# A four-attention chain on one core: the fourth attention's residual and norm moved to token-major rows, epsilon moved into the sum of squares, the last tail in halves, a new order

## What is computed

```python
# block 0: self-attention (sa), strided cross-attention (ca), feed-forward (f), each followed by a LayerNorm
# block 1 (l1): cross-attention, update, LayerNorm:
x4 = (x - mu) * rsqrt(var + 1e-05) * ln_gamma + ln_beta
# block 2 (l2, g): causal cross-attention, residual with its input, LayerNorm, feed-forward
sim = softmax(where(causal, Q @ K^T / sqrt(8), -1e9))
att_h = (sim @ V) + x4                    # V = ctx @ Wv.T + bv
mu, var = mean(att_h), mean((att_h - mu) ** 2)
x5 = (att_h - mu) * rsqrt(var + 1e-05) * ln_g + ln_b
x6 = gelu(x5 @ W1.T + b1) @ W2.T + b2 + x5
# block 3 (l3): attention with squared relu scores in a band, no softmax, then the output
out = x6 + (w / max(sum(w), 1e-06)) @ V @ Wo.T
```

## Time and profile before

| | before |
|---|---|
| median of 3 runs | 197.07 us (196.1 to 197.6) |
| the profiled execution's own time | 196.68 us |
| span of its profile, first to last instruction | 194.7 us |
| granted TensorE clock | 1.000 of full speed |
| busy: PE, PEld | 177.8 us (91%), 134.4 us (69%) |
| busy: DVE, ACT, POOL | 129.3 (66%), 118.1 (61%), 37.5 (19%) us |
| matmul records | 4559 |

### The profile page before, as it was taken

How to read it: one execution, slowest core, us unless ns; L and a number is a source line. 1 busy time by engine, 2 the same in 40 slices (tenths; PEclk the granted TensorE clock), 3 DMA queues, 4 the chain that set the end, 5 groups by cost and what they waited for, 6 DMA issues and landing times.

```text
span 194.7 us, 10288 instructions
## 1 busy us (share of the span) xinstructions
PE 177.8 (91%) x4559; PEld 134.4 (69%) x4559; DVE 129.3 (66%) x251; ACT 118.1 (61%) x307; POOL 37.5 (19%) x65
## 2 busy tenths in 40 slices
PE   7688899988999999999999997979899999999954
PEld 3466577867778699688777574656667677787743
DVE  4899869745865774693679372867855425778850
ACT  3466535774768866567844754365688575757442
POOL 8800007163303024201111100230100101100000
PEclk9999999999999999999999999999999999999999
DMA  5994000000000000000000000000000000000102
GB/s 134 323 389 160 5 3 8 3 3 3 3 3 3 3 3 2 2 3 3 3 3 7 3 5 3 3 3 3 3 5 3 3 3 3 3 0 7 32 3 81
DMA packets 4187, 6.05 MB, mean 31 GB/s; under 512 B 560, under 2 KB 3504, under 8 KB 3888
## 3 DMA queue, kind: packets, MB, share of 16 engines
q1 hardware_dynamic: 3712, 5.23, 8.1%
q10 hardware_dynamic: 432, 0.17, 0.3%
HBM read 4.88 MB, written 0.52 MB: 28 GB/s over the span
## 4 chain that ended last, share of the span: by engine, by line
PE 78%; DVE 7%; issue 6%; ACT 4%; DMA 2%; POOL 0%; ACTq 0%; POOLq 0%
PE bank L334 36%; PE score L337 22%; PE bank L337 12%; PE bank L557 5%; DVE m_col_sb L911 4%; DMA small_sb<-in_small 2%; ACT probs_sb L699 2%; ACT v_ext_sb L683 1%; DVE probs_sb L898 1%; PE bank L467 1%; DVE k_heads_sb L830 1%; DVE q_heads_sb L852 1%; PE bank L415 1%; ACT probs_sb L749 1%; PE bank L620 0%
## 5 line engine op out<-in xcount | busy, mean ns | idle before, releaser
L911 DVE TENSOR_REDUCE m_col_sb<-score 128x32 f32<-128x2048 f32 (+1 forms) x16 | 30.2, 1890 | 11.8 <-PE score L337 11.7
L699 ACT ACTIVATE probs_sb<-score 128x1024 f32<-128x1024 f32 (+1 forms) x28 | 26.2, 963 | 13.1 <-PE score L337 13.0
L334 PEld LDWEIGHTS bank<-v_ext_sb,probs_sb 128*32 128x32 f32 x2176 | 23.1, 110 | 11.4 <-issue 8.5
L334 PE MATMUL bank<-v_ext_sb,probs_sb 128*32 128x18 f32 (+1 forms) x2176 | 27.2, 189 | 2.6 <-issue 1.4
L1042 POOL TENSOR_SCALAR vare_sb<-var_sb 128x2 f32<-128x2 f32 x20 | 7.0, 352 | 106.7 <-ACT att_sb L756 106.7
L337 PE MATMUL score<-q_heads_sb,k_kept_sb 32*64 32x256 f32 x512 | 19.4, 386 | 1.5 <-issue 1.1
L334 PE MATMUL bank<-xa_sb,W_sb 128*128 128x256 f32 x62 | 18.0, 399 | 1.7 <-issue 1.0
L756 ACT ACTIVATE att_sb<-bank 128x128 f32<-128x128 f32 x40 | 10.7, 275 | 10.9 <-PE bank L337 10.8
L557 PE MATMUL bank<-W_sb,att_sb 128*128 128x128 f32 x80 | 16.0, 287 | 0.7 <-DVE att_sb L939 0.4
L1044 POOL TENSOR_TENSOR rstd_sb<-vare_sb,half_sb 128x2 f32<-128x2 f32 x20 | 15.6, 778 | 1.7
L337 PE MATMUL score<-k_heads_sb,q_kept_sb 32*64 32x256 f32 x384 | 13.8, 383 | 2.1 <-issue 1.3
(11 more groups left out here) (143 smaller groups left out, 341.7 us busy)
## 6 DMA issues: line engine op xcount, KB each, us to landing
W_sb<-in_mats SPq DMA_DIRECT2D x1, 1088.0 KB, 8.3
W_sb<-in_mats SPq DMA_DIRECT2D x1, 1024.0 KB, 10.4
ctxT_sb<-in_ctxT SPq DMA_DIRECT2D x1, 512.0 KB, 6.1
cn_sb<-in_ctx SPq DMA_DIRECT2D x1, 512.0 KB, 11.6
hid_sb<-in_idx SPq DMA_DIRECT2D x1, 512.0 KB, 6.7
out<-attT_sb SPq DMA_DIRECT2D x4, 128.0 KB, 1.8
xa_sb<-in_xT SPq DMA_DIRECT2D x2, 128.0 KB, 3.1
xa_sb<-in_xT SPq DMA_DIRECT2D x1, 256.0 KB, 3.9
```

What stands on the lines that cost most here:

```text
L334: return pe.matmul(o, l, r, start=start, stop=stop)
L699: act.activation(dst, src, ACT.Exp, scale=SCALE).then_inc(sem("exp"), 1)
L911: dve.tensor_reduce(o, src, AX.X, ALU.max).then_inc(sem("max"), 1)
```

## The change

Four things are done together.

1. In l2 the steps `flip`, `attT`, `z` and `var` are gone. Instead GpSimd makes the residual token-major: `x4_rows` = `att` of the third norm (scaled, before its transpose) times the gain row plus a bias row, two tensor_tensors of 128x256 for each group. The rows come by a new transfer (`norm_rows`, the last of SyncE's loads) and `row_sum` adds the value bias to them once. `divide/l2` adds `x4_rows` to its product in one more VectorE instruction; a new VectorE step `stats` takes mean and variance of each half by `bn_stats` and `bn_aggr` and adds epsilon; `scale/l2` is two tensor_scalars (minus mean, times `rstd`), SBUF to SBUF.
2. In the other norms epsilon enters as the bias inside the Square, so `rstd` is one GpSimd instruction in place of two.
3. In the last group of l3, `divide`, `flip`, `attT`, `out`, `fin` and `store` are done by halves; the second half of `av` and what follows it lies in `score` and not in the bank.
4. `SCHEDULE` is a new list. Nearly all neighbours change somewhat.

The core of the diff:

```diff
+def split(step, name, g):
+    return g == G - 1 and ((name == "l3" and step in ("av", "divide", "flip", "attT")) or step in ("out", "fin", "store"))
+        def home(step, name, g, i):
+            return score[:, 0, :] if i and split(step, name, g) else bank[g]
...
@@ SyncE
+            sp.dma_start(norm_rows[:].rearrange("p a n -> p (a n)"), a["norm_rows"].to_broadcast([128, 3 * 128])
+                         ).then_inc(sem("norm_rows_loaded"), 16)
@@ TensorE, centred
-                    if name == "l2":
-                        terms = [(here, mat("center"))]
@@ ScalarE, var
                         last = act.activation(att[:, g, j, :], bank[g][:, j * 128:(j + 1) * 128], ACT.Square,
-                                              scale=D ** -0.5, accum_out=var[:, g, j:j + 1])
+                                              bias=eps[:, :], scale=D ** -0.5, accum_out=var[:, g, j:j + 1])
@@ VectorE, divide
+                if name == "l2":
+                    dve.wait_ge(sem("x4_rows"), nth("x4_rows", name, g))
...
+                if name == "l2":
+                    last.then_inc(sem("quotient"), 1)
+                    dve.wait_ge(sem("quotient"), nth_of_layer("divide", name, g))
+                    last = dve.tensor_tensor(att[:, g, :, :], att[:, g, :, :], x4_rows[:, g, :, :], ALU.add)
@@ VectorE, steps
+                elif step == "scale" and name == "l2":
+                    dve.wait_ge(sem("rstd"), nth("rstd", name, g))
+                    for j in range(NJ):
+                        last = dve.tensor_scalar(att[:, g, j, :], att[:, g, j, :], mean_var[:, g, j, 0:1],
+                                                 rstd[:, g, j:j + 1], ALU.subtract, ALU.mult)
...
-                elif step == "attT" and name == "l2":
-                    dve.wait_ge(sem("flip"), nth("flip", name, g))
-                    dve.scalar_tensor_tensor(attT[:, g, :], bank[g][:, 0:GT], col("l2_vb"), X("x4")[:, tok(g)],
-                                             ALU.add, ALU.add).then_inc(sem("attT"), 1)
+                elif step == "stats":
+                    dve.wait_ge(sem("divide"), nth("divide", name, g))
+                    for j in range(NJ):
+                        last = dve.bn_stats(stats[:, g, j, :], att[:, g, j, :])
...
+                    for j in range(NJ):
+                        last = dve.bn_aggr(mean_var[:, g, j, :], stats[:, g, j, :])
...
+                    dve.tensor_scalar(var[:, g, :], mean_var[:, g, :, 1], EPS, None, ALU.add).then_inc(sem("stats"), 1)
@@ GpSimd
+                elif step == "x4_rows":
+                    pool.wait_ge(sem("scale"), nth("scale", "l1", g))
+                    pool.wait_ge(sem("row_sum"), 1)
+                    pool.tensor_tensor(x4_rows[:, g, :, :], att[:, g, :, :],
+                                       norm_rows[:, 0, :].unsqueeze(1).to_broadcast([128, NJ, 128]), ALU.mult
+                                       ).then_inc(sem("x4_scaled"), 1)
+                    pool.wait_ge(sem("x4_scaled"), nth("x4_rows", name, g))
+                    pool.tensor_tensor(x4_rows[:, g, :, :], x4_rows[:, g, :, :],
+                                       norm_rows[:, 1, :].unsqueeze(1).to_broadcast([128, NJ, 128]), ALU.add
+                                       ).then_inc(sem("x4_rows"), 1)
                 elif step == "rstd":
-                    pool.wait_ge(sem("var"), nth("var", name, g))
-                    pool.tensor_scalar(vare[:, g, :], var[:, g, :], EPS, None, ALU.add).then_inc(sem("var_eps"), 1)
-                    pool.wait_ge(sem("var_eps"), nth("rstd", name, g))
-                    pool.tensor_tensor(rstd[:, g, :], vare[:, g, :], half[:, 0:NJ], ALU.pow
+                    pool.tensor_tensor(rstd[:, g, :], var[:, g, :], half[:, 0:NJ], ALU.pow
```

More of the change, by code:

```diff
@@ new lines @@
+ln/ca/1 h/f gelu/f av/ca/2 h/f/1 gelu/f/1 v/ca/3 divide/ca/2 flip/ca/2 attT/ca/2 h/f/0/1 v_even/ca/3 gelu/f/0/1
+k_heads/l1/3 h/f/1/1 v/l1/2 v_odd/l1/2 av/ca/3 k/l2 k_kept/l2 v_even/l1/2 z/ca/2 var/ca/2 rstd/ca/2 gelu/f/1/1 z/f
+k_heads/l1/1 patterns var/f rstd/f divide/ca/3 k_heads/l1/2 k_heads/l2 flip/ca/3 attT/ca/3 z/f/1 row_sum scale/ca/2
+flip_x/ca/2 scale/f flip_x/f var/f/1 rstd/f/1 z/ca/3 ln/f ln/ca/2 var/ca/3 scale/f/1 q/l1 q_kept/l1 h/f/2 s/l1
+flip_x/f/1 gammas rstd/ca/3 scale/ca/3 flip_x/ca/3 gelu/f/2 h/f/2/1 ln/f/1 q/l1/1 ln/ca/3 h/f/3 max/l1 max_parts/l1
@@ new lines @@
+q_kept/l1/1 s/l1/1 gelu/f/2/1 gelu/f/3 m/l1 m_row/l1 z/f/2 var/f/2 rstd/f/2 h/f/3/1 gelu/f/3/1 q_heads/l1 max/l1/1
+max_parts/l1/1 m/l1/1 m_row/l1/1 t/l1 exp/l1 scale/f/2 flip_x/f/2 exp/l1/0/1 z/f/3 var/f/3 k/l2/1 ln/f/2 av/l1
+q_heads/l1/1 k_kept/l2/1 t/l1/1 exp/l1/1 rstd/f/3 scale/f/3 q/l1/2 av/l1/0/1 divide/l1 q_kept/l1/2 q_heads/l1/2
+ctx_rows//1 flip_x/f/3 k_heads/l2/1 ctx_normed//1 exp/l1/1/1 k/l2/2 k_kept/l2/2 flip/l1 attT/l1 av/l1/1 s/l1/2 z/l1
+ln/f/3 q/l1/3 var/l1 rstd/l1 max/l1/2 av/l1/1/1 ctx_rows//2 q_kept/l1/3 s/l1/3 divide/l1/1 ctx_normed//2
@@ new lines @@
+max_parts/l1/2 m/l1/2 m_row/l1/2 k/l2/3 k_kept/l2/3 scale/l1 flip_x/l1 ln/l1 flip/l1/1 attT/l1/1 max/l1/3 k/l3/2
+k_kept/l3/2 k_heads/l2/2 ctx_rows//3 q_heads/l1/3 q/l2 q_kept/l2 max_parts/l1/3 ctx_normed//3 t/l1/2 q_heads/l2
+exp/l1/2 k_heads/l2/3 exp/l1/2/1 z/l1/1 var/l1/1 av/l1/2 av/l1/2/1 s/l2 divide/l1/2 rstd/l1/1 scale/l1/1 flip_x/l1/1
+x4_rows/l2/1 ln/l1/1 m/l1/3 m_row/l1/3 ctx_rows ctx_normed max/l2 flip/l1/2 attT/l1/2 q/l2/1 q_kept/l2/1
+q_heads/l2/1 v/l3 v_even/l3 v_odd/l3 x4_rows/l2 t/l1/3 exp/l1/3 exp/l1/3/1 z/l1/2 var/l1/2 rstd/l1/2 k/l3 k_kept/l3
@@ new lines @@
+av/l1/3 s/l2/1 max_parts/l2 m/l2 scale/l1/2 k/l3/1 k_kept/l3/1 flip_x/l1/2 av/l1/3/1 max/l2/1 v/l3/1 ln/l1/2
+v_even/l3/1 max_parts/l2/1 q/l2/2 m_row/l2 t/l2 q_kept/l2/2 v_odd/l3/1 divide/l1/3 flip/l1/3 attT/l1/3 v/l2
+v_even/l2 exp/l2/0/1 v/l3/2 z/l1/3 v/l2/1 exp/l2 v_even/l3/2 var/l1/3 q_heads/l2/2 rstd/l1/3 s/l2/2 v_even/l2/1
+v_odd/l2 av/l2 v_odd/l2/1 scale/l1/3 flip_x/l1/3 v_odd/l3/2 max/l2/2 av/l2/0/1 divide/l2 x4_rows/l2/2 stats/l2
+ln/l1/3 m/l2/1 m_row/l2/1 q/l2/3 q_kept/l2/3 t/l2/1 exp/l2/1/1 exp/l2/1 rstd/l2 max_parts/l2/2 m/l2/2 m_row/l2/2
@@ new lines @@
+divide/l2/3 gelu/g/1/1 y/g/1 x6/g/1 stats/l2/3 ln/l2/2 h/g/2 square/l3/0/1 q/l3/1 q_heads/l3/1 rstd/l2/3 square/l3
+av/l3 scale/l2/3 gelu/g/2 h/g/2/1 gelu/g/2/1 t/l3/1 gate/l3/1 flip_x/l2/3 ln/l2/3 y/g/2 square/l3/1 h/g/3 gelu/g/3
+x6/g/2 x_sq/l3/2 q/l3/2 gate/l3/1/1 q_heads/l3/2 av/l3/0/1 divide/l3 h/g/3/1 x_sq/l3/1 ms/l3/1 floor/l3/1 gelu/g/3/1
+t/l3/2 gate/l3/2/1 y/g/3 square/l3/1/1 av/l3/1 flip/l3 x6/g/3 q/l3/3 x_sq/l3/3 av/l3/1/1 attT/l3 out square/l3/2/1
+gate/l3/2 fin ms/l3/2 q_heads/l3/3 square/l3/2 t/l3/3 divide/l3/1 flip/l3/1 floor/l3/2 av/l3/2 gate/l3/3 ms/l3/3
@@ L151 @@
+attT/l3/1 out//1 store gate/l3/3/1 floor/l3/3 av/l3/2/1 divide/l3/2 square/l3/3 fin//1 store//1 av/l3/3 divide/l3/3
+flip/l3/2 square/l3/3/1 av/l3/3/1 divide/l3/3/1 flip/l3/3 attT/l3/2 out//2 attT/l3/3 fin//2 store//2 flip/l3/3/1
+attT/l3/3/1 out//3 fin//3 store//3 out//3/1 fin//3/1 store//3/1
 """
@@ L637, in _ @@
                 elif step == "flip":
[L638 removed]
+                    flip("flip", name, g, i, "divide")
                 elif step == "z":
@@ L641, in _ @@
                 elif step == "flip_x":
-                    flip("flip_x", name, g, "scale")
+                    flip("flip_x", name, g, i, "scale")
                 elif step == "h":
```

187 lines of the change are left out of this document (100 added, 87 removed).

## The result

The changed kernel takes **188.2 us** (median, 186.8 to 189.1) where the kernel before took 196.9 us beside it on the same chip (196.1 to 197.6): a ratio of 0.955, 95% interval 0.947 to 0.963. It is 8.7 us faster.

What follows compares the result with a forecast made beforehand. TensorE was taken as the bound, through its work and its idle moments. Terms 3.0 + 0.8 + 1.3 + 0.3 - 1.1 = 4.3 us off 196.7 gave 192.4, plus 0.4 made 192.8 us; range 190.0 to 197.0.

Steps and rivals of the forecast that it cites:

- TensorE's work: In l2, six matmul records fewer per group, 24 in all: 3.0 us saved, bounds 2.9 and 3.3.
- epsilon: In 16 norms GpSimd loses an add of 0.35 us, mostly hidden: 0.3 us saved, bounds 0 and 1.0.
- The tail: Last group of l3 by halves: shorter transpose, output, copies and divide save 0.8 us, bounds 0.5 and 1.1.
- the pause's 1.3: TensorE's 1.34 us instruction pause between halves of group 1's output disappears: 1.3 us saved, lower bound 0.
- the first rival: The tail's pause stays or moves to as bad a place: 194.1 us, chance 0.13.
- The five other pauses: TensorE's mid-step instruction pauses outside the tail fall elsewhere in the new order: counted as no change.
- The new order closes other pauses too: Rival: half of TensorE's five remaining pauses go, 2.2 us more saved: 190.6 us, chance 0.10.
- The rule of the Trainium skill: Instruction blocks of 16 KB or 256, crossing cost mostly hidden; if so, the tail's pause may stay, saving 1.3 us less.
- TensorE's saving turns into waits: Rival: the 3.0 us stay unseen as TensorE waits anyway, and the tail's pause reappears elsewhere: 196.0 us, chance 0.20.
- VectorE's added work: In l2, net 1.1 us more per group on VectorE, 4.4 us for four, range 3.4 to 5.5.
- A quarter visible, 1.1 us: Of VectorE's 4.4 us more work, a quarter shows as TensorE waits: 1.1 us lost, bounds 0 and 4.4.
- GpSimd's rows: Two added l2 instructions per group at 1.2 us each, just hidden under TensorE: 0; at the upper bound TensorE waits 2.8.

Runs made afterwards that it cites:

- n_e_off: The changed kernel with epsilon added by GpSimd again for the 16 norms outside l2: 188.6 us, ratio 0.959 to the kernel before.
- o_all: The kernel before, in its old order, with token-major l2 norm, tail halves and epsilon edit all put in: ratio 0.992 to the kernel before.
- o_t: The kernel before, in its old order, with the token-major l2 norm as the only edit: ratio 0.988 to the kernel before.

## Why the prediction was wrong

**The bound** (TensorE, and the moments in which it stands still) was right; no other engine came to bound anything.

The sum, term by term, in the profiled executions. The prediction took 3.5 us off TensorE's work and 1.3 off its pauses, and let the other waits rise by 0.5 (1.1 for VectorE, less 0.3 for epsilon and 0.3 for the tail's shorter copies and divide): 4.3. Measured were 2.5, 3.7 and 1.4 less: 7.6.

**TensorE's work**, 3.0 us and 0.5 in the tail's transpose and output, came out as 2.5 us of busy time. Records and place were right, the size 1.0 too large.

**The tail** was right. 2.1 us were counted for halves and pause together, and up to the last `fin` 2.3 were measured: 1.34 for the pause and 0.9 for the rest, where 0.8 was forecast with a bound of 1.1. The 0.3 us less behind the last `fin` were not in the sum. But there was luck in the pause's 1.3: the block end now lies 116 records from the end, in the last `av`, and cost 0.35 us in the profile; in `n_e_off` and with 256 instructions ahead a pause at the same count costs 1.43 us. So the first rival, a pause in as bad a place, was nearer than its 0.13. The halves of `attT` and `fin` take 0.27 and 0.28 us, the 0.1 less that was assumed.

**The five other pauses** are the step that failed: "The other five I leave as they are: they fall elsewhere in the new order, and I have no ground to count them up or down." Counting them at no change was a statement on their sum, with no width given to it. Pauses of all sizes fell by 3.7 us, the one in the tail among them, so 2.4 us more than counted. (Nor were there five: the view of waits has ten idle times put down to issue, 7.1 us in all, so the tail's apart 5.8 us were left standing.) The runs with shifted blocks show how wide that term is: the sum goes from 3.3 to 12.1 us in one and the same list of instructions, and the time with it by 13 us, part of it from the half clock behind some of the long pauses. The rival "The new order closes other pauses too", with 0.10 and 190.6 us, was the right mechanism, and its chance was far too small; "Nothing in the rows says that it would" was true, but nothing said that it would not. The range had to reach some 5 us down from the forecast and more than that up.

**The rule of the Trainium skill** that was weighed (Runtime: NRT & Kernel Launch, Instruction fetch mechanics) names the block of 256 instructions, and the runs agree with that size: 256 ahead restore the time, and in the changed kernel 36 to 128 do not. "Mostly hidden" holds by number, as of 36 or 37 block ends no more than 5 to 13 show as idle time in the ten traces. By time it is not small here: what shows adds up to 3.3 to 13.6 us, 2 to 7% of the span.

**The other waits** are the second step that failed: they fell by 1.4 us where the sum let them rise by 0.5. The order did this. `o_all` and the changed kernel hold the same edits and the same 4535 records, with block ends at the same counts within two, and differ in order alone: spans 194.1 and 187.1 us, of which 3.1 are other waits, 1.7 are pauses put down to issue and 2.2 busy time (`o_all` has its tail at half clock). Of the 3.1, 1.4 are its wait for the divide that I had placed badly. The edits alone, in the old order, did not: there the rival "TensorE's saving turns into waits" is what `o_t` shows for groups 0 and 1. The forecast had put the new order itself at 0. What share the order would have had with other places for the norm's steps stays open.

**VectorE's added work** was priced well for most and put at 4.4 us; its busy time rose by 5.6. The groups by line, after (busy and mean ns):

```profile
L1032 DVE BATCH_NORM_STATS2 stats_sb<-att_sb 128x6 f32<-128x128 f32 x8 | 1.9, 284 | 0.1
L983 DVE TENSOR_TENSOR att_sb<-att_sb,x_rows_sb 128x256 f32<-128x256 f32 x4 | 1.7, 425 | 0.1
L1036 DVE BATCH_NORM_AGGREGATE mean_var_sb<-stats_sb 128x2 f32<-128x6 f32 x8 | 1.0, 166 | 0.1
L1104 POOL TENSOR_TENSOR x_rows_sb<-att_sb,norm_rows_sb 128x256 f32<-128x256 f32 x4 | 2.9, 727 | 0.8 <-DVE att_sb L1025 0.8
```

Three of the prices (0.28, 0.42, 0.155) are met within some 0.01 us. The scale was not: 0.28 was taken, and it has 0.34 alone and up to 0.88 (next section). "A quarter visible, 1.1 us" was nearly right by luck: it meets the 1.2 us wait for L1020 above, which is one wait and not a share, and comes from a slowdown that was not foreseen (last section).

**GpSimd's rows** take 0.73 us each, not 1.2, and TensorE waits for none of l1's norms behind them: the term 0 was right. The sum for it was not as it was called: 6.8 us against 6.6 of cover is 0.2 short, not "just hidden"; with 0.73 us for each instruction it is 4.9 us and hidden.

**What is left when the offset is taken out.** At offsets 0, 36, 84 and 128 the medians average 199.2 us before and 194.7 after, 4.6 apart; by the lowest times it is 5.1 (198.6 and 193.5). At equal offsets the gap runs from 9.1 us to 3.2 us the other way. In the two profiles at full clock the span without its issue pauses is 187.6 before and 183.7 after, 3.9 apart, where the sum without its pause term gave 3.0. So some 4 to 5 us belong to the steps and their order, and the rest of the 8.7 to where the blocks end. Four offsets are few, some medians rest on one or two executions, and the pairs at 36 and 128 were run on different chips, so this is no more than an idea of size.

## What to carry to other kernels

- When a kernel issues small matmuls in dense runs, count where its instruction blocks end before believing a gain or loss of some per cent: adding or dropping instructions anywhere ahead shifts every later end, and moving them changes what lies on one. Test a change at two or three offsets, by splitting work that is hidden at the start, and against a shift by one whole block.
- A removed round trip is worth its engine time only where the order has something to put in its place; in the old order the norm's edit saved 2.2 us of TensorE's busy time, and 0.6 us of that came back as other waits.
- A term without ground for up or down is not zero with no width: its spread belongs in the range.
